# Output weights loaded ahead of the second stacking, the first body's second swap ahead of its first stacking, and another drain order

## The reference

```
x = x + 0.5 * _L0_ffn_ref(_layernorm(x), router_w, router_b, A, Bm)
x = x + _L0_attn_ref(_layernorm(x), wq_a, q_norm_w, wq_b, wkv_a, kv_norm_w, wkv_b, wo)
x = x + 0.5 * _L0_ffn_ref(_layernorm(x), router_w, router_b, A, Bm)
```

## Time and profile before

| what | value |
|---|---|
| median of 3 runs | 2177.68 us (2177.6 to 2181.52) |
| the profiled execution | 2180.48 us, its span 2178.7 us |
| PE busy | 2123.7 us, 97% of the span |
| DVE, ACT, POOL busy | 73%, 63%, 57% |
| one body of pair 0, start to start | 60.2 us |
| granted TensorE clock, mean | 0.998 of full speed |

### The profile page before, as it was taken

One profiled execution on the slowest core, in us unless ns is written; L12 is line 12 of the kernel. 1 busy time (PEld: TensorE's weight loads), 2 busy tenths in 40 slices (PEclk: granted clock), 3 DMA queues, 4 the chain that ended last, 5 costly groups with the idle time before them and its releaser, 6 DMA issues.

```text
span 2178.7 us, 44641 instructions
## 1 busy us (share of the span) xinstructions
PE 2123.7 (97%) x11548; PEld 1802.3 (83%) x11548; DVE 1585.4 (73%) x3415; ACT 1371.0 (63%) x3561; POOL 1247.1 (57%) x1643
## 2 busy tenths in 40 slices
PE   8989999999999999999899999999999999999998
PEld 7977888888888888888688978888888888888877
DVE  7667777777777777778787667777777777777777
ACT  6556666666666666666665566666666666666664
POOL 5336666666776666666554355555555555555543
PEclk9999999999999999999999999999999999999999
DMA  4034444443334444445423133333333333333331
GB/s 164 19 79 142 137 146 136 145 127 120 104 119 138 146 135 142 146 155 165 147 79 121 52 101 115 114 114 114 114 114 114 114 114 114 114 114 114 111 98 78
DMA packets 221201, 258.02 MB, mean 118 GB/s; under 512 B 145872, under 2 KB 174672, under 8 KB 219088
## 3 DMA queue, kind: packets, MB, share of 16 engines
q1 hardware_dynamic: 216528, 244.64, 36.7%
q10 hardware_dynamic: 4608, 12.58, 1.7%
HBM read 127.14 MB, written 79.69 MB: 95 GB/s over the span
## 4 chain that ended last, share of the span: by engine, by line
PE 65%; DMA 10%; POOL 9%; issue 5%; DVE 4%; ACT 3%; SPq 3%; POOLq 0%; ACTq 0%; DVEq 0%
PE ps L890 50%; DMA stage<-in_wo 7%; PE ps L969 5%; PE ps L1302 4%; PE ps L1246 2%; DMA arena<-arena 2%; PE ps L916 1%; DMA stage<-stage 1%; POOL arena L2703 1%; PE ps L904 1%; SPq L781 1%; POOL stage L2704 1%; POOL stage L2698 1%; ACT arena L1463 1%; ACT stage L1837 1%
## 5 line engine op out<-in xcount | busy, mean ns | idle before, releaser
L2412 DVE TENSOR_TENSOR xacc<-ps,xacc 128x512 f32<-128x512 f32 x896 | 603.0, 686 | 190.9 <-PE ps L890 177.1
L2021 DVE TENSOR_TENSOR arena<-ps,arena 128x512 fp32r<-128x512 f32 (+4 forms) x744 | 425.3, 577 | 202.0 <-ACT arena L1463 201.7
L890 PE MATMUL ps<-arena,extra 128*128 128x512 f32 x1920 | 522.6, 401 | 5.7 <-DVE xacc L2412 5.4
L1828 ACT ACTIVATE stage<-ps,negmax 128x128 f32<-128x128 f32 (+6 forms) x512 | 260.2, 508 | 339.3 <-DVE negmax L2391 332.7
L1463 ACT ACTIVATE arena<-ps 128x512 fp32r<-128x512 f32 (+4 forms) x744 | 369.3, 506 | 137.9 <-PE ps L890 57.3
L890 PE MATMUL ps<-zT,arena 128*128 128x512 f32 (+1 forms) x1746 | 446.3, 400 | 1.9 <-DVE arena L2021 1.0
L890 PEld LDWEIGHTS ps<-arena,extra 128*128 128x128 f32 x1920 | 341.7, 188 | 88.8 <-DVE xacc L2412 17.9
L890 PEld LDWEIGHTS ps<-zT,arena 128*128 128x128 f32 x1746 | 317.6, 189 | 68.8 <-ACT stage L1463 1.3
L2716 POOL TENSOR_TENSOR extra<-extra_plain,extra 128x256 fp32r<-128x256 f32 (+1 forms) x256 | 223.4, 875 | 164.8 <-ACT extra L1463 164.4
L890 PE MATMUL ps<-arena 128*128 128x512 f32 x960 | 262.1, 408 | 14.2 <-POOL arena L2716 7.9
L890 PE MATMUL ps<-keyT,arena 128*128 128x192 f32 (+5 forms) x1152 | 265.7, 339 | 3.6 <-ACT stage L1828 3.6
(11 more groups left out here) (129 smaller groups left out, 3117.9 us busy)
## 6 DMA issues: line engine op xcount, KB each, us to landing
kept_b<-arena SPq DMA_DIRECT2D x16, 3584.0 KB, 11.2
arena<-kept_b SPq DMA_DIRECT2D x112, 512.0 KB, 6.1
arena<-arena SPq DMA_DIRECT2D x128, 128.0 KB, 3.0
stage<-in_wo SPq DMA_DIRECT2D x32, 512.0 KB, 13.2
stage<-stage SPq DMA_DIRECT2D x248, 64.0 KB, 2.0
extra<-arena SPq DMA_DIRECT2D x120, 128.0 KB, 3.0
kept_q<-arena SPq DMA_DIRECT2D x16, 768.0 KB, 11.1
arena<-kept_q ACTq DMA_DIRECT2D x32, 384.0 KB, 6.6
```

What stands on the lines that cost most here:

```text
L890: last = nc.tensor.matmul(dst, w, m, start=start and n == 0, stop=stop and n == len(passes) - 1, skip_group_check=skip)
L1828: nc.scalar.activation(prob[u][:, poff(u, i):poff(u, i) + w], bank_s(i)[:, 0:w], ACT.Exp, bias=negmax[:, k % 2, i:i + 1], accum_out=rowsum ...
L2021: return nc.vector.tensor_tensor(dst, src, part.bitcast(F32), ALU.subtract)
L2412: nc.vector.tensor_tensor(xs, bank_y(k, j), xs, ALU.add).then_inc(y_added, 1)
```

## The change

It touches all five engines; no instruction that computes is added or removed.

- `body`, pair 0, SP: the waits of `split_b(g)` and `load_wo(g + 1)` stand in front of the second `stack_halves`; `keep_b(g)` stays behind it.
- `first_body`, pair 0, SP: the swap of `pf1` stands in front of the first `stack_halves`, whose landing SP now waits for. On POOL the sums of unit 2 up to `s3` stand in front of `split_wpe`, on ACT the first `split_a` of that unit moves up to `valued`, and on DVE B11's low part stands in front of the sum T2.
- `first_body`, pair 1, SP: the swap of `pe0` stands in front of the stacking of `pf1`'s part.
- `drained`, both pairs, all engines: turns, output products, norms, splits and adds in another order.

```diff
                 if early:
                     load_early(g, 2)
@@ body, SP
+                if p == 0 and not last:
+                    landed_wqn(g + 1)
+                if p == 0:
+                    split_b(g)
+                    if not last:
+                        load_wo(g + 1)
                 if early:
                     load_early(g, 3)
                 if not last:
                     stack_halves(turns(p, g, 1) + 1, 0, 4 * slot_n(p, g, 2))
                 if p == 0:
-                    if not last:
-                        landed_wqn(g + 1)
-                    split_b(g)
                     kept(g - 1)
                     keep_b(g)
-                    if not last:
-                        load_wo(g + 1)
-                    else:
+                    if last:
                         kept(g)
@@ first_body, SP
-                stack_halves(r, 1, None, 0, PART, landed=False)
-                sp.wait_ge(q_act, qbase(p, 0) + ev["pf1"][0] + 1)
-                swap_halves(PART, SEQ)
...
+                    sp.wait_ge(rope_ready, r)
+                    sp.wait_ge(q_act, qbase(p, 0) + ev["pf1"][0] + 1)
+                    swap_halves(PART, SEQ)
+                    stack_halves(r, 1, None, 0, PART)
+                    stack_halves(r + 1, 1, None, PART, SEQ, landed=False)
...
+                    sp.wait_ge(rope_ready, r + 1)
+                    sp.wait_ge(q_act, qbase(p, 0) + ev["pe0"][0] + 1)
+                    swap_halves()
+                    stack_halves(r + 1, 1, None, PART, SEQ)
+                    landed_wpe(p, 1)
@@ drained, PE
-                turn_probs(n, 3, 0, False)
-                turn_probs(n, 3, 1, False)
-                turn_probs(n, 3, 2, False)
-                out_(0, 0, 1, 2, 3)
-                turn_probs(n, 3, 3, False)
-                out_(0, 4, 5)
+                for i in range(4):
+                    turn_probs(n, 3, i, False)
+                out_(0, 0, 1, 2, 3, 4, 5)
                 values(n, 3, False)
...
-                out_(1, 0)
+                out_(1, 0, 1)
                 pe.wait_ge(ra_hi, s + 1)
                 pe.wait_ge(ra_lo, s + 1)
                 up(0)
-                out_(1, 1, 2, 3)
+                out_(1, 2)
+                up(1)
                 turn_ffn(s, 2)
-                up(1)
-                out_(1, 4, 5)
+                out_(1, 3, 4)
                 turn_ffn(s, 3)
-                out_(1, 6)
+                out_(1, 5, 6)
@@ first_body, POOL
                 if p == 0:
+                    sums(unit_n(p, 0, 2), steps="124a3")
                     split_wpe(p, 1)
-                sums(unit_n(p, 0, 2), y_n(p, 0, 2) if p else None)
+                    sums(unit_n(p, 0, 2), steps="bc")
+                else:
+                    sums(unit_n(p, 0, 2), y_n(p, 0, 2))
```

More of the change, by code:

```diff
@@ L680, in first_body @@
                     landed_wqn(1)
[L681 to L684, removed]
+                    landed_wpe(p, 1)
+                    sp.wait_ge(q_act, qbase(p, 0) + ev["pe0"][0] + 1)
+                    swap_halves()
+                    stacked(r + 1)
+                else:
+                    stack_halves(r, 1, None, 0, PART, landed=False)
+                    sp.wait_ge(q_act, qbase(p, 0) + ev["pf1"][0] + 1)
+                    swap_halves(PART, SEQ)
+                    for j in range(3, NPROD):
+                        b_again(0, j)
+                    stacked(r)
+                    sp.wait_ge(rope_ready, r + 1)
+                    sp.wait_ge(q_act, qbase(p, 0) + ev["pe0"][0] + 1)
+                    swap_halves()
+                    stack_halves(r + 1, 1, None, PART, SEQ)
+                    landed_wpe(p, 1)
                 if p == 0:
@@ L1658, in first_body @@
                     norms(p, 0, 1, 3)
-                    valued(slot_n(p, 0, 0), whole=False)
+                    valued(slot_n(p, 0, 0))
                     fills("q3")
@@ L1965, in drained @@
                 split_a(n - 1, 1)
+                turned(n, 3, 2)
                 split_a(n - 1, 2)
-                turned(n, 3, 2)
                 turned(n, 3, 3)
@@ L1974, in drained @@
                 norm_ffn(s, 1)
+                split_a(n, 1)
                 turned_ffn(s, 0)
-                split_a(n, 1)
+                turned_ffn(s, 1)
                 split_a(n, 2)
-                turned_ffn(s, 1)
+                keep_h(F0[s])
                 norm_ffn(s, 2)
[L1980 to L1987, removed]
+                norm_ffn(s, 3)
+                turned_ffn(s, 2)
+                keep_h(F0[s] + 1)
+                norm_ffn(s, 4)
+                turned_ffn(s, 3)
+                norm_ffn(s, 5)
+                keep_h(F0[s] + 2)
+                turned_ffn(s, 4)
+                keep_h(F0[s] + 3)
+                turned_ffn(s, 5)
+                norm_ffn(s, 6)
+                gates(F0[s] // HT)
+                keep_h(F0[s] + 4)
+                norm_ffn(s, 7)
+                turned_ffn(s, 6)
+                split_bm(s)
             def attention(p):
@@ L2705, in rotate, with sums @@
                 G.tensor_tensor(low, both, high.bitcast(F32), ALU.subtract).then_inc(rope_ready, 1)
-            def sums(m, used=None, all_first=False):
+            def sums(m, used=None, steps="124a3bc"):
                 a11, a12, a21, a22 = (operand(name, 1, 1, True) for name in ("a11", "a12", "s3", "a22"))
@@ L2785, in body @@
                     split_t(g, T1)
-                sums(unit_n(p, g, 2), y_n(p, g, 2), all_first=p == 0)
+                sums(unit_n(p, g, 2), y_n(p, g, 2), steps="1243abc" if p == 0 else "124a3bc")
                 if p == 0:
@@ L2814, in drained @@
                 sums(unit_n(s - 1, NG, 0), y_n(s - 1, NG, 0))
-                for i in range(NT):
-                    ln_ffn(s, i)
-                    if i == 1:
-                        sums(unit_n(s - 1, NG, 1), y_n(s - 1, NG, 1))
-                    if i >= 3:
-                        add_h(F0[s] + i - 3)
+                ln_ffn(s, 0)
+                ln_ffn(s, 1)
+                sums(unit_n(s - 1, NG, 1), y_n(s - 1, NG, 1))
+                ln_ffn(s, 2)
+                ln_ffn(s, 3)
+                add_h(F0[s])
+                ln_ffn(s, 4)
+                ln_ffn(s, 5)
+                add_h(F0[s] + 1)
+                add_h(F0[s] + 2)
+                ln_ffn(s, 6)
+                add_h(F0[s] + 3)
+                ln_ffn(s, 7)
                 if s == 1:
                     ln_ffn(s, NT)
+                add_h(F0[s] + 4)
             G.memset(neg_half[:, :], -0.5).then_inc(half_ready, 1)
```

64 lines of the change are left out of this document (30 added, 34 removed).

## The result

The changed kernel takes 2163.01 us (median of 4 runs, 2162.06 to 2163.68) against 2178.23 us for the kernel before in the same comparison (4 runs, 2177.6 to 2181.52). The ratio is 0.9927, with a 95% interval of 0.9913 to 0.9941: 15.2 us faster. The prediction was 2160.6 us in a range of 2156.5 to 2168, so the range holds it.

What follows compares the result with a forecast made beforehand. PE, busy 97%, bounds the kernel, its repeated wait being for the output weights' load. Terms 12.0 + 3.4 + 0.7 + 1.0 = 17.1 us take the median from 2177.68 to 2160.6 us, range 2156.5 to 2168.

Steps and rivals of the forecast that it cites:

- The loop: Pair 0's loop: the stall for the output weights goes, 0.86 us a body, fourteen times, 12.0 us; bounds 6 to 13.
- (c) of term 1: Pair 0's loop: rotary weights load and later swaps come earlier, with 1.1 MB less in front; no gain or loss.
- a rival: Bodies 14 and 15: swaps stop delaying POOL, and the drains give 3 us; 2156 us, chance 0.05.
- I let the stacking land 1.2 us later: Pair 0's loop: stacking behind the moved load lands in 4.2 us against 3.0, with 6 us to spare.
- The cover of (b): Pair 0's loop: write of the products lands at 547.8, ACT's copy of `m0` needs it at 550.0; 2.2 us left.
- The slow rival: Every loop body: late stacking delays the write and ACT's `m0` copy, priced fourteen times; 2182 us at 4.9 later, chance 0.03.
- Pair 0's first body: Earlier swap and new order remove PE's 2.60 us POOL wait and the lowered clock: 3.4 us; bounds 1 to 4.
- The swap was to land 1.8 us sooner: Pair 0's first body: swap issued 2.7 us earlier, lands 1.8 us earlier, so POOL starts at 144.0.
- Half a microsecond was to come back at `pe0`: Pair 0's first body: fill `pe0` needs the split now behind the sums, 152.9 against PE's 152.4.
- Pair 1's first body: Swap of `pe0` ahead of the stacking shortens PE's 1.15 us POOL wait: 0.7 us; bounds gain 1.1, loss 1.
- The drains: Both drains: four transposes fall into a 0.64 us wait; 0.5 us each, 1.0 us; bounds loss 2, gain 3.
- the rest trades places among waits of the same kind: Drains: apart from the last turn's four transposes, the reordering was given no gain of its own.

Runs made afterwards that it cites:

- run 1: Kernel before with only SyncE's loop body changed (load of the output weights in front of the second stacking): 2169.4 us, ratio 0.9946.
- run 2: Changed kernel with SyncE's loop body as before, so first bodies and drains alone: 2176.51 us, ratio 0.998.
- Run 3: Kernel before with the load of the output weights between the second stacking and the write of the products: 2172.16 us, ratio 0.9962.
- run 5: Changed kernel with two unused 1 MB DRAM copies between load and second stacking in each loop body of pair 0: 2173.12 us.
- run 4: Changed kernel with one unused 1 MB DRAM copy between load and second stacking in each loop body of pair 0: 2163.29 us.
- run 6: Kernel before with only SyncE's new order in pair 0's first body (swap ahead of first stacking): 2179.21 us.
- run 10: Changed kernel with pair 1's head loads and the write of `kept_q` moved behind the second swap in pair 0's first body: 2171.24 us, ratio 0.996.
- run 7: Kernel before with only the new orders of POOL, VectorE and ScalarE in pair 0's first body: 2179.05 us.

## Why the prediction came out as it did

**The loop, 12.0 us predicted, 12.2 measured.** The mechanism holds: run 1 shows it alone, run 2 the rest without it. The size is right in part by luck. I read the 14 waits of the earlier trace rows as 14 bodies. There were 13 stalls in the loop, of 0.79 us each on average where I had costed one body at 0.86: 10.2 us, not 12.0. The other 2.0 us come from the last two bodies (1.2, of which 0.1 is the last stall, and 0.9), which I had named only as a little more in the bounds and as a rival, while (c) of term 1 put them at nothing. There POOL's swap stood in the queue behind the write and the load:

```profile
976.94 1.29 POOL L2698 TENSOR_TENSOR stage<-stage,pos_tab 128x512 f32<-128x512 f32 x1 [4.72 <-DMA stage<-stage]
...
985.85 1.65 PE L890 MATMUL ps<-arena 128*128 128x512 f32 x6 [0.45 <-POOL arena L2716]
...
1038.66 1.28 POOL L2698 TENSOR_TENSOR stage<-stage,pos_tab 128x512 f32<-128x512 f32 x1 [3.88 <-DMA stage<-stage]
```

In the other loop bodies POOL waited 2.5 to 2.8 us for the same swap. With the change it waits in none. Run 3 keeps all these waits and has no stall for the load: its loop bodies lose 0.1 us, for the write, so waits of 2.5 to 3.0 us are covered, while the last two bodies, with 3.9 and 4.7, are longer before.

**What is late next.** I let the stacking land 1.2 us later because it did so behind the load in the first body. In the loop it lands in 3.0 us as before. The reason is the distance. In the first body its first copy leaves 1.7 us behind the last part of the load (167.93 and 169.60) and lands 0.6 us behind it (173.2 and 173.8). In the loop of the changed kernel it leaves 2.9 us behind it (283.09 and 285.97), and the load lands at 288.6, 0.4 us before the copy does. The write lands in 10.5 us besides, not 11.2. The cover of (b) is 4.5 us and not 2.2. The slow rival was priced wrongly as well. It took every microsecond past the cover as lost fourteen times; run 5 is 0.85 us past it on average and pays 0.23 us a body, and more only in the bodies at the end. I had weighed a rule of the Trainium skill ("DMA: Bandwidth & Descriptors", section "Queues, rings and completion order"): a semaphore increment on a DMA engine lands only behind that engine's earlier writes. The traces agree: in none of the places above does the stacking land ahead of the load in front of it, and in runs 4 and 5 the write that waits for the stacking leaves 2.8 and 5.1 us later behind 1 and 2 MB. For the load alone it costs nothing in the loop.

**Pair 0's first body, 3.4 us predicted, 2.5 measured** on the stretch. The wait for POOL is gone, and the clock with it, as said. The swap was to land 1.8 us sooner; it did so by 1.0 alone in run 6. Half a microsecond was to come back at `pe0`; it was 1.19, and the step that failed is whose it would be: I looked at POOL's split and not at VectorE, whose split of `B21` ends at 153.67, behind POOL's at 153.55.

**Pair 1's first body, a gain of 0.7 us predicted, a loss of about 0.9 measured.** The step that failed is that the swap's new place "takes it off a chain of POOL steps that PE waits 1.15 us for". There was little to free. The swap needs ScalarE's copy of `pe0`: before, that ends at 1272.29 and the swap leaves at 1272.70; after, 1256.81 and 1256.88. And POOL's third step of the rotation needs the stacking landed too, which now follows the swap:

```profile
1264.61 1.29 POOL L2718 TENSOR_TENSOR arena<-stage 128x512 fp32r<-128x512 f32 x1 [1.56 <-DMA extra<-arena]
...
1271.67 1.65 PE L899 MATMUL ps<-arena 128*128 128x512 f32 x6 [2.11 <-POOL arena L2731]
```

From PE's nine-matmul fill there (1258.90, after 1242.94) to this row, seven executions with the old order take 27.03 to 28.59 us, mean 27.86, with a wait of 1.15 to 2.42. Five with the new one take 28.36 to 29.28, mean 28.76. The earlier trace rows was the shortest of the seven waits. In two of the five (runs 2 and 10) the clock fell behind the wait, which costs about 1.6 us more past that row; in none of the seven it did. The part was not undone by itself, so this rests on two groups of executions that differ in other things too.

**The drains, 1.0 us predicted, 3.0 measured** (1.55 and 1.5). The step I had priced came out as said: the 0.64 us wait of the earlier trace rows fell to 0.19. What I put at nothing, "the rest trades places among waits of the same kind", is mis-sized. In drain 1 all idle stretches of PE that the timeline marks sum to 4.0 us before and 3.4 after. The rest of the 1.55 us lies in PE's rows themselves, which are shorter where they are not split (eight transposes in one row 1.09 us, four and four 0.63 and 0.60). No run takes the drain's edits apart.

**The total.** 17.1 us was predicted and 15.2 measured between medians. By parts the traces give 12.2, 2.5, -0.9 and 3.0, and 1.1 for the clock in drain 2, against 12.0, 3.4, 0.7 and 1.0. So the total is closer than its terms: the first bodies gave 2.5 us less and the drains 2.0 more than I said. What is left lies in how executions of one kernel differ. The start varies by 2 us (the same PE row at 109.12 to 111.33), and pair 1 from the first to the second drain, with no edit in it, takes 992.2 us in run 1 and 988.8 in the kernel before.

## What to carry to other kernels

A small load that a queue issues behind a large write pays for the write (13.3 us instead of 4.9 here), so put it ahead of the write. The place further forward is worth having for what it does to the write and to the small copies behind the write, not to the load. Count the waits by place before you multiply one of them: 14 in a sum over the span were 13 of one kind and one of another. Before a step is moved past another, list what each consumer's instruction waits for (the rotation waited for two transfers, not for one), and do not take one execution's wait as its size when it hangs on a transfer. Two edits that shorten the same chain are not two gains: run each alone.

## What the runs showed that I had not expected

- **The clock.** The length of a stop alone does not tell whether the granted clock falls. Behind 2.75, 2.60, 2.56 and 2.18 us in pair 0's first body it fell (the nine matmuls at 2.9 to 3.7 us instead of 2.3, the window of 156 to 158 us before at 0.50), behind 1.43 it did not. In pair 1's first body it fell behind 2.13 and 2.12 us and not behind 2.42, 2.32, 2.12, 2.11 or 2.08. In drain 2 the same stop of 0.83 and 0.84 us was followed by six matmuls of 2.75 us once and 1.67 the other time.
- **The start.** Its 2 us are the clock as well. At about 37 us, in the first feed-forward stage, the granted clock is 0.50 for a stretch in four of the 14 traces (runs 1, 3, 5 and 7). These four have the PE row named above at 110.95 to 111.33 us, the other ten at 109.12 to 109.89.
- **ScalarE's slack.** Where its copy of `m0` comes 0.93 and 0.85 us late on average, PE loses 0.1 and 0.23 us a body (runs 3 and 5).
- **The write itself.** The same 3.5 MB land after 10.5, 11.2 or 13.9 us, depending on whether the load is long through, behind it, or right in front of it.
